# Perceiver cross attention: the weighted sum over the context is turned round

## The reference

```python
# b = 16, n = 64 latents, s = 1024 context rows, DIM = 256, 16 heads of 64
lat = layer_norm(latents) * ln_lat_g + ln_lat_b
ctx = layer_norm(context) * ln_ctx_g + ln_ctx_b
q = heads(lat @ Wq);  k, v = heads(split(ctx @ Wkv))
k = apply_rope(k, cos, sin)          # halves of a head: x1*cos - x2*sin, x2*cos + x1*sin
attn = softmax(clip(q @ k.T * scale, -11, 11))
out = (attn @ v) @ Wo + bo           # heads joined again
x = x + out
x = x + linear_attention(_layernorm(x))
x = x + mixture_of_experts(_layernorm(x))
```

## Time and profile before

| | us |
|---|---|
| three executions | 1292.77, 1293.83 (median), 1295.97 |
| profiled execution, first to last instruction (span) | 1292.6 |
| TensorE busy | 1269.5 (98%) |
| VectorE busy | 980.8 (76%) |
| ScalarE busy | 621.5 (48%) |
| GpSimd busy | 606.4 (47%) |

### The profile page before, as it was taken

How to read it: one execution, slowest core, us unless ns; L and a number is a source line. 1 busy time by engine, 2 the same in 40 slices (tenths; PEclk the granted TensorE clock), 3 DMA queues, 4 the chain that set the end, 5 groups by cost and what they waited for, 6 DMA issues and landing times.

```text
span 1292.6 us, 43933 instructions
## 1 busy us (share of the span) xinstructions
PE 1269.5 (98%) x18292; PEld 1136.7 (88%) x18292; DVE 980.8 (76%) x1973; ACT 621.5 (48%) x1264; POOL 606.4 (47%) x611
## 2 busy tenths in 40 slices
PE   7999999999999999999999999999999999999997
PEld 4788998899889889988999899889988878789997
DVE  7887787787778777877787777777766456668886
ACT  6344444444444454445444544454444333346664
POOL 3565554564455555545654555455443123323333
PEclk8999999999999999999999999999999999999999
DMA  6253343434343434343443434343454360556662
GB/s 221 62 122 88 95 116 85 108 75 121 80 108 77 121 79 108 80 117 82 106 114 88 108 76 116 87 108 75 112 122 108 79 228 31 179 174 189 187 189 82
DMA packets 71509, 145.56 MB, mean 113 GB/s; under 512 B 18248, under 2 KB 45584, under 8 KB 69136
## 3 DMA queue, kind: packets, MB, share of 16 engines
q1 hardware_dynamic: 67232, 138.53, 40.7%
q0 software_dynamic: 4080, 4.22, 1.6%
HBM read 61.74 MB, written 14.76 MB: 59 GB/s over the span
## 4 chain that ended last, share of the span: by engine, by line
PE 94%; DVE 1%; DMA 1%; ACT 1%; issue 1%; POOL 0%; SPq 0%; POOLq 0%; ACTq 0%; DVEq 0%
PE bank L1346 29%; PE bank L1380 10%; PE bank L1382 9%; PE bank L1381 9%; PE bank L1332 9%; PE bank L1646 6%; PE bank L1392 4%; PE bank L1362 2%; PE bank L1353 2%; PE bank L1477 2%; PE bank L1696 1%; PE bank L1698 1%; PE bank L1697 1%; PE bank L1503 1%; PE bank L1546 1%
## 5 line engine op out<-in xcount | busy, mean ns | idle before, releaser
L505 POOL TENSOR_TENSOR kr<-kr,ksw 128x1024 f32<-128x1024 f32 x128 | 318.5, 2488 | 449.4 <-DVE pr L863 345.7
L1380 PE MATMUL bank<-x_hi,p_hi 128*128 128x258 f32 x1024 | 300.9, 294 | 0.0
L1382 PE MATMUL bank<-x_hi,p_lo 128*128 128x258 f32 x1024 | 288.5, 282 | 0.0
L1381 PE MATMUL bank<-x_lo,p_hi 128*128 128x256 f32 x1024 | 287.8, 281 | 0.0
L1346 PE MATMUL bank<-ct_hi,wk_hi 128*128 128x512 f32 x512 | 213.5, 417 | 1.3 <-DVE kr L895 1.1
L884 DVE TENSOR_TENSOR kw<-bank,stab 128x1024 f32<-128x1024 f32 x128 | 156.7, 1224 | 61.0 <-PE bank L1346 60.9
L617 ACT COPY o_part<-bank 128x64 f32<-128x64 f32 x128 | 27.2, 213 | 362.5 <-PE bank L1392 362.5
L1346 PE MATMUL bank<-ct_hi,wk_lo 128*128 128x512 f32 x512 | 201.3, 393 | 0.0
L1346 PE MATMUL bank<-ct_lo,wk_hi 128*128 128x512 f32 x512 | 200.6, 392 | 0.0
L863 DVE TENSOR_SCALAR pr<-pr 128x1024 f32<-128x1024 f32 x128 | 90.1, 704 | 139.8 <-ACT pr L621 139.7
L1381 PEld LDWEIGHTS bank<-x_lo,p_hi 128*128 128x128 f32 x1024 | 194.7, 190 | 0.0
(11 more groups left out here) (220 smaller groups left out, 2180.8 us busy)
## 6 DMA issues: line engine op xcount, KB each, us to landing
ksw<-kw SPq DMA_DIRECT2D x512, 128.0 KB
raw<-in_ctx_dram SPq DMA_DIRECT2D x16, 1024.0 KB, 6.1
w_two<-in_L_ffn_W_dram SPq DMA_DIRECT2D x15, 1024.0 KB, 4.9
x_slots<-fill SPq DMA_DIRECT2D x128, 64.5 KB, 3.1
w_all<-in_L_ffn_W_dram SPq DMA_DIRECT2D x4, 2048.0 KB, 15.6
wo<-in_L_ffn_W_dram SPq DMA_DIRECT2D x7, 1024.0 KB, 5.0
xs<-x_slots SPq DMA_DIRECT2D x23, 129.0 KB, 2.2
raw<-in_x_dram SPq DMA_DIRECT2D x4, 512.0 KB, 4.6
```

The source lines that it names most:

```text
L505: pool.tensor_tensor(kr[:, i], kr[:, i], ksw[:, i], ALU.add).then_inc(kr_done, 1)
L1380: pe.matmul(psZ[:, 0:D + 2], p_hi[:, i, c], x_hi[:, b, t], start=(t == 0), stop=False, skip_group_check=True)
L1381: pe.matmul(psZ[:, 0:D], p_hi[:, i, c], x_lo[:, b, t], start=False, stop=False, skip_group_check=True)
L1382: last = pe.matmul(psZ[:, 0:D + 2], p_lo[:, i, c], x_hi[:, b, t], start=False, stop=(t == ST - 1), skip_group_check=True)
```

## The change

The weighted sum is turned round. The context rows are now stationary (`xc`, 128 rows by 128 features) and the weights move, 512 columns at a time: two halves of two pairs of heads each. A step is no longer one pair on 1024 context rows but two pairs on 512 rows (`pairs_of`, `half_of`), and four steps make a quad: four pairs on all 1024 rows. The sum comes out transposed (features by latents), in two banks `psZ[0]` and `psZ[1]`, so that the transposes of `zn` and the copies around them are gone. Sum number j runs in step j + 2, one bank for an even j and the other for an odd one.

The outputs are done once for each quad (32 matmuls in a row, `outputs`, in steps 7, 11, 15, ...). They are divided by the denominators only at the end: the last feature of the context rows is replaced by ones (and zeros in the low part), row 127 of the second half of the sum `zt` is then the denominator, two small DMAs spread it over 128 partitions (`lsum`), and VectorE takes the reciprocal of 128 by 256 elements and multiplies. Since a normalised row sums to nought, the last feature is minus the sum of the others, which goes into `wv` (`value_weights`). The gain of the context norm goes into the key and value weights, its shift into a bias for each key column (`kbias`) and into the freed last row of `wv`; eight matmuls ahead of the loop (`biases`) and ten small DMAs make these. A context tile so takes one pass (`normalised`) in place of two. The rotation products become `scalar_tensor_tensor` instructions, (key + bias) by table, on 512 columns: four a step in place of two on 1024.

TensorE's order in a step becomes scores, keys, outputs (every fourth step), weighted sum, turning of a context tile eight steps ahead. VectorE does the first half of the rotation ahead of the low part of the weights, and the second half behind it. The context is loaded in halves (512 KB in place of 1 MB), one every four steps.

The core of the diff (TensorE first, then VectorE, and at the end one wait each of SyncE and GpSimd):

```diff
             def step(j):
...
-                if there(j - 2):
-                    for k in range(KC):
-                        last = pe.transpose(psZT[:, k * P:(k + 1) * P], zn[:, k * P:(k + 1) * P], ident[:])
-                    last.then_inc(zt_ps, 1)
-                if there(j - 1):
-                    for t in range(ST):
-                        c = slice(t * P, (t + 1) * P)
-                        pe.matmul(psZ[:, 0:D + 2], p_hi[:, i, c], x_hi[:, b, t], start=(t == 0), stop=False, skip_group_check=True)
-                        pe.matmul(psZ[:, 0:D], p_hi[:, i, c], x_lo[:, b, t], start=False, stop=False, skip_group_check=True)
-                        last = pe.matmul(psZ[:, 0:D + 2], p_lo[:, i, c], x_hi[:, b, t], start=False, stop=(t == ST - 1), skip_group_check=True)
-                    last.then_inc(z_ps, 1)
...
+                scores(j)
+                keys(j + 2)
+                outputs(j)
+                sums(j - 2)
...
+                turn_context(j + 8)
+            def keys(j):
+                    for a, g in enumerate(pairs_of(j)):
+                        wait(pe, ku_done, 2 * (j - 1) + a + 1)
+                        if a == 0:
+                            pe.wait_ge(ct_lo_done, HT * (h + 1))
...
+                        last.then_inc(k_ps, 1)
+            def sums(j):
+                    pe.wait_ge(p_lo_done, 2 * h + 2)
...
+                    parts = [(t, l, r) for t in range(HT) for l, r in ((0, p_hi), (1, p_hi), (0, p_lo))]
+                    for m, (t, l, r) in enumerate(parts):
+                        last = pe.matmul(psZ[c], xc[:, slot_, l, t, cols], r[:, i, t], start=(f == 0 and m == 0), stop=(f == 1 and m == len(parts) - 1),
+                                         skip_group_check=True)
+                    last.then_inc(z_ps, 1)
...
+            def outputs(j):
+                if due(j, 7):
...
+                    dve.tensor_tensor(o_part[:], psO[0], o_part[:], ALU.add).then_inc(o_sum, 1)
+                    dve.wait_ge(lsum_ld, 32 * (n + 1))
+                    dve.reciprocal(lsum[:], lsum[:]).then_inc(o_sum, 1)
+                    dve.wait_ge(o_sum, 2 * n + 2)
+                    dve.tensor_tensor(qo[:, g:g + 4, at:at + N], o_part[:].rearrange("p (g n) -> p g n", n=N),
+                                      lsum[:].rearrange("p (g n) -> p g n", n=N), ALU.mult).then_inc(o_done, 1)
+            def keys_turned(j, a):
+                    dve.scalar_tensor_tensor(out=kw[:, i, cols], in0=psK[:, cols], scalar=kbias[:, g:g + 1], in1=stab[:, places],
+                                             op0=ALU.add, op1=ALU.mult).then_inc(kw_done, 1)
+                    dve.scalar_tensor_tensor(out=kr[:, i, cols], in0=psK[:, cols], scalar=kbias[:, g:g + 1], in1=ctab[:, places],
+                                             op0=ALU.add, op1=ALU.mult).then_inc(ku_done, 1)
...
             def step(j):
+                normalised(j)
+                counted(j)
+                moments_taken(j)
+                clamped(j)
+                keys_turned(j, 0)
+                weights_low(j)
+                keys_turned(j, 1)
+                outputs(j)
+                context_low(j)
...
             def step(j):
-                    wait(sp, kw_done, j + 3)
+                    sp.wait_ge(kw_done, 2 * (j + 3))
...
             def step(j):
-                    wait(pool, ku_done, j + 2)
+                    pool.wait_ge(ku_done, 2 * (j + 2))
```

More of the change, by code:

```diff
@@ L534, in _ @@
             constants()
-            for j in range(-12, 0):
-                step(j)
-            for j in range(STEPS):
+            for j in range(-5, STEPS):
                 step(j)
@@ L673, in _ @@
             key_weights(1)
-            for g in range(PAIRS):
+            for g in range(7):
                 queries(g, 0)
@@ L1114, in _ @@
             normalise(0, 0)
[L1115 to L1117 removed]
+            outputs(STEPS + 3)
             constants()
@@ L1487, in turn @@
                 last.then_inc(xnT_ps, 1)
-            for j in range(STEPS + 2):
+            for j in range(2, STEPS):
                 step(j)
-                if j == STEPS:
-                    turn(0)
+            step(STEPS)
+            turn(0)
+            step(STEPS + 1)
+            project_heads(2, 0, 2)
+            outputs(STEPS + 3)
             project_heads(2, 2, 4)
```

732 lines of the change are left out of this document (383 added, 349 removed).

## The result

| | before | after |
|---|---|---|
| median of the executions, us | 1293.39 | 1361.47 (1358.26 to 1372.62) |
| ratio, 95% interval | | 1.054 (1.050 to 1.058) |
| profiled span, us | 1292.6 | 1360.6 |
| start of the scores of step 2 | 64.3 | 73.6 |
| start of the last scores | 1012.7 | 1074.9 |

The forecast was 1257 us with a range to 1288. The kernel became slower by 68 us: 9.3 ahead of step 2, 52.9 in the loop (125 times 0.42) and 5.8 behind it.

The account below looks back on a forecast made before the run. TensorE, busy for 98% of the span, was taken to bound the kernel at 7.59 us a step. Its gain of -56, +8 for keys, +7 for late swaps and +4 for start and end gave -37: 1257 us, range 1238 to 1288.

Parts of the forecast that it names:

- TensorE's part: TensorE's matmuls in the loop: mean step from 7.59 to 7.15 us, 0.44 a step, 56 us gained.
- The scalar_tensor_tensor: VectorE's rotation products with bias from PSUM on 512 columns: 0.75 us each, bounds 0.62 and 0.97.
- The normalisation in one pass: VectorE's normalising of a context tile: one instruction of 0.41 us in place of two.
- The swap in the step shown: Swap of the halves of `kw` by SyncE's DMAs: taken at 4.4 us, fitting by 0.6 us.
- The step that failed: VectorE's order within a step: products to 4.3, low part of the weights to 5.4, second `kw` to 6.1 us.
- Within one step it does once: VectorE bounds once in eight steps: keys wait 0.55 us for the context tile's low part behind the division, +8 us.
- Both are hidden: SyncE's context loads and `lsum` DMAs, and ScalarE's changed copies, were to cost no time.
- Late swaps, +7: GpSimd's add waits for a swap of 6.15 us in 25 / 105 of the steps, 0.24 a step: +7 us.
- The rival with late swaps everywhere: Second rival: swaps are late in all steps as more DMAs share the queue, +31, 1281 us; chance 0.17.
- Start and end, +4: Ahead of the loop and behind it: bias matmuls, `value_weights` passes and the last `lsum` wait, +4 us.
- The fourth rival: Slower: rotation products at 1.10 us make VectorE the bound, 7.73 us a step, 1315 us; chance 0.07.
- the prediction's own signs of being wrong: TensorE waiting in most steps, sums starting further apart than 0.25 us, or VectorE without idle time ahead of its clamp.

Follow-up runs that it names:

- The fastest kernel (1272.7): Against the kernel of 1275.0, SyncE's load of `lsum` is issued behind the swap of `kw`, not ahead of it: 1272.7 us, ratio 0.984.
- the measurement of two engines: Not the kernel: each kind of VectorE instruction run six times alone and six times while GpSimd adds 1024-column tiles, writing zeros; 158 us.
- the one where the rest is mended: The kernel of 1275.0 with `p_lo` again between the halves of the rotations: 1355.1 us; with `p_lo` replaced by an instruction reading PSUM: 1291.2 us.
- e11_xc_first: The kernel of 1275.0 with ScalarE's copy of `xc` put back ahead of its copy of `o_part`: 1292.9 us, ratio 1.000.
- e2_copy_first: The kernel after with ScalarE's copy of the outputs ahead of its copy of `xc` in steps with outputs: 1341.3 us, ratio 1.039.
- e12_divide_whole: The kernel of 1275.0 with the division whole again and ahead of `ct_low`: 1309.9 us, ratio 1.013.
- e4_loads_later: The kernel after with SyncE's 23 small loads issued one a step from step 3 on, not ahead of the first swap: 1358.6 us, ratio 1.049.
- the kernel of 1275.0: The kernel after with `o_part` copied before `xc`, small loads later, `p_lo` behind rotations and outputs' addition, reciprocal halved behind `ct_low`: 1275.0 us, ratio 0.986.

## Why the prediction was wrong

**TensorE's part** had the right kind and too large a size. The sums are 12 matmuls 0.228 us apart and the turning of `zn` is gone. But a plain step takes 6.99 against 6.88 (scores 1.09 for 1.04, turning 0.32 for 0.22), and one with outputs 8.31 against 7.98, where the keys take 2.95 and the sum 2.87 instead of 2.85 and 2.73. The sum in the prediction took the pace within a run of one shape; here a run next to another shape takes about 0.1 us more, at its first or its last matmul. TensorE's own rows give (3 x 6.99 + 8.31) / 4 = 7.32 us a step, 0.27 and not 0.44 below before, so 34 us where -56 stood. The fastest kernel (1272.7) gives 30.9 us back in the loop (917.5 us for 125 steps against 948.4), with 4.6 lost ahead of it and 3.1 behind: that is what the turned sum is worth here with its order mended.

The scalar_tensor_tensor (0.744 against 0.75) and the reciprocal (1.744 against 1.7) are right. The normalisation in one pass, taken at 0.41, has a median of 0.404 and a mean of 0.536; it is a tensor_scalar of 256 columns in SBUF, of the kind that the measurement of two engines shows stretched. The swap in the step shown is 4.35 us against 4.4 (`kw` ends at 517.6 and the add starts at 521.92), but that is a short one: where an add waited for it (200 to 1000 us), the add started 5.4 us behind the end of `kw` in the median.

**The step that failed** is the timing within VectorE's step: "then come two products to 4.3, the low part of the weights to 5.4, the second `kw` to 6.1". In the step at 500.00 this held to the tenth (`p_lo` ends at 5.43, `kw` at 6.10). But `p_lo` was taken at 1.24 from a trace in which it nearly always ran when GpSimd's add was over. The change moves it into the add: in the kernel after 59 of the 128 start before an add of `kr` is over. I had the place of the add and the new order of VectorE on the same page and did not lay one beside the other. Before's own trace even holds the price: of 128 `p_lo`, three start before an add of `kr` is over, two of them in its last 0.5 us (1.46 and 1.51 us long), and the third, with 1.4 us of the add to go, takes twice its time.

```profile
1007.46 2.36 POOL L505 TENSOR_TENSOR kr<-kr,ksw 128x1024 f32<-128x1024 f32 x1 [5.20 <-DVE pr L863]
...
1008.44 2.46 DVE L910 TENSOR_TENSOR p_lo<-pr,p_hi 128x1024 fp32r<-128x1024 f32 x1 [1.11 <-ACT p_hi L637]
```

The mean of the group, 1237 ns, does not show it; its longest would have. The term for this in the sum was zero. It is 36 us in the kernel after and 64 in the one where the rest is mended. These are parts of more than the 68 us: from the 1272.7 of the mended order to the 1361.5 of the kernel after are 89, and the causes overlap, so the parts need not add up.

**"Within one step it does once"** (8 us for keys behind the division) was the right mechanism with the wrong size. I had the outputs' addition end at 7.1. In every second outputs step it ended at 9.4, since ScalarE's queue holds the `xc` copy ahead of it. I had written of ScalarE "Both are hidden" from its busy time and had not asked for what each of its copies waits. That is 18 to 20 us (e11_xc_first, e2_copy_first). The wait of the keys came once in eight steps, as forecast, but was 0.95 us and not 0.55: 11.4 us in 100 steps, 14 in the loop by that pace, against 8. Where the rest is mended, the whole division ahead of the low part costs 35 us (e12_divide_whole).

**Late swaps, +7.** The add waited for the swap in 66 of 100 steps and not in a quarter. The swaps were no slower than those that an add waited for before (5.4 us in the median against 6.0), but they started later: `kw` was whole 6.9 us behind the scores in the mean, and not 6.1. The rival with late swaps everywhere names the symptom (1281) and not the cause.

**Start and end, +4** (bounds -3 and +10), came out at 9.3 and 5.8, 15.1 together and outside the bounds. The bias matmuls were not at fault; ten DMAs for them, and loads that stood behind those, kept SyncE from the first swap, and moving the loads gave 5.5 us of the 9.3 back (e4_loads_later). At that wait TensorE's clock was at its lower level as well (0.50 from 56.00 to 62.70 us), so the first scores took 1.92 us and not 1.09. At the end VectorE waits 4.4 us for the last `lsum` (L953's idle time above), where some 3 were expected.

**The fourth rival** had the right side and the wrong engine event: it asked whether the rotations get long enough for VectorE to be the bound on the mean. They don't touch the contention at all, and VectorE is busy for 82% only. The largest part of the loss that is measured comes from one instruction at the wrong moment. Of the prediction's own signs of being wrong, VectorE without idle time ahead of its clamp showed in half: the clamp waited for the exponential in 51 of 100 steps, before in all. The matmuls of a sum did not start further apart.

## What to carry to other kernels

When an instruction moves on VectorE, look at what GpSimd does in the window that it moves into: with two operands in SBUF (or as a tensor_scalar from SBUF to SBUF) it did not run beside GpSimd's add here, with one in PSUM it did, and the profile shows the wait as a longer duration and not as idle time. Compare the longest of a group with its mean before taking the mean. For an in-order queue, list what each instruction waits for, not only how long all of them take; and when several causes are mixed, mend them all first and put them back one at a time, since taking single ones out gave 26, 20, -39 and 3 us (the last within the spread), and putting them back 80, 18 and 35.

## What the runs showed of the hardware

- VectorE beside GpSimd: 1.25 to 3.30 us for two SBUF operands of 1024 columns, 0.72 to 2.72 and 0.44 to 2.40 for tensor_scalar of 1024 and 256 columns, nothing with a PSUM operand. GpSimd's add is the one that grows when it starts second (3.40 us from 504.30 on in the kernel after, behind a `p_lo` that began at 504.21; 2.4 undisturbed).
- A reciprocal of 256 columns takes 1744 ns; with 163 for one column that is 6.2 ns a column.
- A swap of four SBUF to SBUF DMAs keeps SyncE's queue for 2.42 us, and for 4.06 where the two `lsum` DMAs went just ahead (at 514.77 us in the kernel of 1275.0).
- TensorE's granted clock fell to 0.50 at some of TensorE's waits (here one of 1.71 us ahead of 491.41 in the kernel after), and stayed at 1.00 in the loop of the kernel before, which has none. Keys that take 2.85 us at full clock took 4.44, part of them at the lower level.
